# A paged-attention pipeline in which the turning of queries and keys moves from TensorE to VectorE, and projection and output products are dealt out anew over the units of a round

## The reference, cut to what matters

```python
q = rope(rmsnorm(x @ Wq.T, q_norm_w), pos)        # 32 heads of 128
k = rope(rmsnorm(x @ Wk.T, k_norm_w), pos)        # 8 heads of 128
v = x @ Wv.T
k_all = concatenate([k_cache[block_table], k])    # 512 cached keys + 32 new ones
v_all = concatenate([v_cache[block_table], v])
probs = softmax(where(valid, q @ k_all.T * SCALE, -1e30))
y = (probs @ v_all).reshape(...) @ Wo
```

## Time and profile before

| | us |
|---|---|
| median of 3 runs (3074.37 to 3078.14) | 3076.71 |
| the profiled execution | 3076.38 |
| its span, first to last instruction | 3074.7 |

### The profile page before, as it was taken

How to read it: one execution, slowest core, us unless ns; L and a number is a source line. 1 busy time by engine, 2 the same in 40 slices (tenths; PEclk the granted TensorE clock), 3 DMA queues, 4 the chain that set the end, 5 groups by cost and what they waited for, 6 DMA issues and landing times. The chain is left out here.

```text
span 3074.7 us, 54713 instructions
## 1 busy us (share of the span) xinstructions
PE 2931.6 (95%) x14616; PEld 1941.9 (63%) x14624; DVE 1527.6 (50%) x4189; ACT 1241.4 (40%) x2633; POOL 1459.5 (47%) x1262
## 2 busy tenths in 40 slices
PE   5889999999999999999999999999999998799997
PEld 3566666666666666666666666666666665455554
DVE  4544444444444444444444444444444444577675
ACT  2444444444444444444444444444444442122222
POOL 4555555555555555555555555555555551000000
PEclk9999999999999999999999999999999999899998
DMA  8544444444444444645444444444444444321110
GB/s 304 182 118 122 121 122 121 122 121 121 121 121 121 121 121 121 203 121 166 131 121 121 121 121 121 119 121 119 121 119 120 121 119 149 98 46 53 41 43 14
DMA packets 433387, 369.66 MB, mean 120 GB/s; under 512 B 90598, under 2 KB 371178, under 8 KB 432186
## 3 DMA queue, kind: packets, MB, share of 16 engines
q1 hardware_dynamic: 377834, 187.06, 21.5%
q0 software_dynamic: 48320, 165.48, 16.9%
q10 hardware_dynamic: 7056, 14.53, 1.3%
HBM read 335.66 MB, written 22.81 MB: 117 GB/s over the span
## 5 line engine op out<-in xcount | busy, mean ns | idle before, releaser
L558 DVE CUSTOM_DVE_ANT_0 ps_s<-ps_s,mask 128x544 f32<-128x544 f32 x512 | 374.9, 732 | 931.6 <-PE ps_s L388 919.3
L463 ACT ACTIVATE ps_s<-ps_s,nmax 128x544 f32<-128x544 f32 x512 | 352.3, 688 | 870.6 <-DVE nmax L558 868.4
L288 POOL DMA_INDIRECT v_sb<-in_v_rows_w,v_row x504 | 488.3, 969 | 449.6 <-PE ps_oT L416 240.5
L347 PE MATMUL ps_t<-wqkv,xT 128*128 128x512 f32 x1488 | 700.5, 593 | 0.0
L411 PEld LDWEIGHTS ps_oT<-pT,v_sb 128*128 128x128 f32 x4096 | 528.7, 192 | 192.6 <-issue 174.9
L411 PE MATMUL ps_oT<-pT,v_sb 128*128 128x128 f32 x4096 | 544.7, 276 | 12.9 <-DMA v_sb<-in_v_rows_w,v_row 12.8
L371 PE MATMUL ps_t<-wo,oT 128*128 128x512 f32 x1024 | 521.9, 594 | 1.5 <-ACT oT L477 1.2
L387 PE MATMUL ps_s<-k_sb,qT 128*128 128x416 f32 x1024 | 447.3, 519 | 19.1 <-issue 12.4
L569 DVE TENSOR_SCALAR p_sb<-ps_s,rinv 128x512 f32<-128x512 f32 x512 | 384.5, 751 | 26.9 <-DVE rinv L566 0.3
L396 PEld LDWEIGHTS ps_pT<-ident_sb,p_sb 128*128 128x128 f32 x2048 | 251.8, 141 | 187.5 <-issue 184.1
L347 PEld LDWEIGHTS ps_t<-wqkv,xT 128*128 128x128 f32 x1488 | 254.4, 191 | 178.0 <-issue 178.0
(11 more groups left out here) (224 smaller groups left out, 3305.5 us busy)
## 6 DMA issues: line engine op xcount, KB each, us to landing
k_sb<-in_kT SPq DMA_DIRECT2D x2048, 64.0 KB
v_sb<-in_v_rows_w,v_row POOLq DMA_INDIRECT x512
wo<-in_wo_w POOLq DMA_DIRECT2D x2, 4096.0 KB, 14.5
v_new<-v_raw SPq DMA_DIRECT2D x512, 16.0 KB, 1.8
y_scratch<-y_sb SPq DMA_DIRECT2D x32, 256.0 KB, 2.3
xT<-x1T_scratch POOLq DMA_DIRECT2D x31, 256.0 KB, 4.9
wqkv<-in_wqkv_w ACTq DMA_DIRECT2D x6, 1024.0 KB, 12.2
wqkv<-in_wqkv_w POOLq DMA_DIRECT2D x6, 1024.0 KB, 12.8
```

What stands on the lines that cost most here:

```text
L288: e.indirect_dma_start(out=v_sb[:, b % 2, c, :], out_offset=None, in_=A["v_rows_w"], in_offset=bass.IndirectOffsetOnAxis(ap=v_row[:, b, c: ...
L347: m = e.matmul(ps_t[bank_of(t)][:, :], xT[:, k, :], wqkv[:, k, 512 * t:512 * t + 512], start=k == 0, stop=k == KC - 1)
L463: e.activation(scores(u), scores(u), ACT.Exp, bias=nmax[:, u % 2:u % 2 + 1], scale=-1.0, accum_out=rsum[:, u % 2:u % 2 + 1]).then_inc(expe ...
L558: e.tensor_tensor_reduce(out=scores(u), in0=scores(u), in1=mask[:, b % 2, :], scale=-SCALE, scalar=3e38, op0=ALU.add, op1=ALU.min, accum_o ...
```

## The change

- **Projection** is dealt out product by product: 24 products over units 0 to 6, as 4, 3, 4, 3, 4, 3, 3 (`PROJECT_TO`), again some before and some behind `turn_p`. `DONE_AT` says in which unit each tile ends; ACT's `raw_copy` and DVE's `sums` follow one unit later.
- **Output products** stand two a unit in units 7 to 13 and one in 14 and 15. In the last round they stand two a unit in units 2 to 9.
- **Turning** leaves PE and ACT: `turn_q`, `copy_q` and the tiles `qT` and `kT_new` go. DVE turns instead: for each of the 4 sequences 4 instructions, each of which takes 32 rows and 32 columns of all 20 heads (32 x 640 elements) from `rot` to `qkT`. They stand in units 11 to 15 (two, two, one, two, one) and, of the next round, in units 0 to 2 (three, three, two), some before `norm` and some behind it.
- **`rotate`**: part 0's scale, power and product are now done tile by tile, 4 heads each, as each tile is summed. The order on POOL is otherwise as before.
- **`embed`**: the block ahead of it goes, its two loads come behind the first loads of x on SP. The projection's weights are issued by SP, one tile in each of the groups 0 to 5, in place of all six by ACT. DVE dequantises ahead of the first `spread`.
- **`tail`**: the last round's output products are made in `tail`, 11 ahead of the first transposes and 5 behind them, from `o_last`, which lies in the weights' region. The loads at its head go to POOL and split into those at once and those after the products; two of the seven instructions of `split_low_rank` go, since a mask and an identity in `B2g` let the product make the whole sum.
- The second half's projection weights count on one semaphore, so tile 0 of round 16 waits for all six.

The diff, cut to its core:

```diff
-STEPS, STEPS1 = 15, 6
+STEPS, STEPS1, RSTEPS = 17, 8, 8
+TURNS = D // S
+def blocks_turned(r, b):
+    return NQT + TURNS * GB * (r - 1) + TURNS * (b + 1)
...
-        self.qT = sb("qT", [P, 2, HKH, GB, REP, S], F32)
-        self.kT_new = sb("kT_new", [P, HKH, P], F32)
+        self.qkT = sb("qkT", [P, GB, HT, S], F32)
... rotate
-    e.wait_ge(W.summed, NQT * r + tiles)
-    e.tensor_scalar(ss[:, h0:h1], ss[:, h0:h1], 1.0 / D, EPS, ALU.mult, ALU.add).then_inc(rstd_step, 1)
-    e.tensor_tensor(rstd[:, h0:h1], ss[:, h0:h1], mhalf[:, h0:h1], ALU.pow).then_inc(rstd_step, 1)
-    e.tensor_tensor(raw[:, h0:h1, :], raw[:, h0:h1, :], rstd[:, h0:h1].unsqueeze(2).broadcast_to([P, n, D]), ALU.mult).then_inc(rope_step, 1)
+    for t0, t1 in ((0, 1), (1, 2), (2, 3)) if i == 0 else ((3, NQT),):
+        a, b = 4 * t0, 4 * t1
+        e.wait_ge(W.summed, NQT * r + t1)
+        e.tensor_scalar(ss[:, a:b], ss[:, a:b], 1.0 / D, EPS, ALU.mult, ALU.add).then_inc(rstd_step, 1)
+        e.tensor_tensor(rstd[:, a:b], ss[:, a:b], mhalf[:, a:b], ALU.pow).then_inc(rstd_step, 1)
+        e.tensor_tensor(raw[:, a:b, :], raw[:, a:b, :], rstd[:, a:b].unsqueeze(2).broadcast_to([P, b - a, D]), ALU.mult).then_inc(rope_step, 1)
... tables
-    TURN_AT = {8: 0, 9: 1, 10: 2, 11: 3, 12: 4}
-    OUT_AT = {6: (0, 2), 7: (2, 4), 8: (4, 5), 9: (5, 7), 10: (7, 8), 11: (8, 10), 12: (10, 11), 13: (11, 13), 14: (13, 14), 15: (14, 16)}
+    TURN_AT = {11: (1, 1), 12: (1, 1), 13: (1, 0), 14: (1, 1), 15: (1, 0), 0: (1, 2), 1: (1, 2), 2: (1, 1)}
+    TURN_NEXT = sum(sum(TURN_AT[u]) for u in range(11, 16))
+    PROJECT_TO = (0, 4, 7, 11, 14, 18, 21, 24)
+    DONE_AT = {u: t for t in range(NT) for u in range(7) if PROJECT_TO[u] < KC * t + KC <= PROJECT_TO[u + 1]}
+    OUT_AT = {u: (2 * u - 14, min(2 * u - 12, HQH)) for u in range(7, 14)}
+    OUT_AT.update({14: (14, 15), 15: (15, 16)})
+    LAST_OUT_AT = {u: (2 * u - 4, 2 * u - 2) for u in range(2, 2 + HQH // 2)}
... PE
+            def parts(r, n0, n1):
+                for t in range(NT):
+                    k0, k1 = max(n0 - KC * t, 0), min(n1 - KC * t, KC)
+                    if k0 < k1:
+                        project(r, t, k0, k1)
...
-                    if u < NT and not last(r):
-                        project(r + 1, u, 0, 2)
+                    if u < len(PROJECT_TO) - 1 and not last(r):
+                        half = PROJECT_TO[u] + 2
+                        parts(r + 1, PROJECT_TO[u], half)
...
-                    if u in TURN_AT and not last(r):
-                        turn_q(r + 1, TURN_AT[u])
...
-                    if u < NT and not last(r):
-                        project(r + 1, u, 2, KC)
+                    if u < len(PROJECT_TO) - 1 and not last(r):
+                        parts(r + 1, half, PROJECT_TO[u + 1])
...
-            out_product(ROUNDS - 1, 1, 0, HQH)
... ACT
-                    if 1 <= u <= NT and not last(r):
-                        raw_copy(r + 1, u - 1)
+                    if u - 1 in DONE_AT and not last(r):
+                        raw_copy(r + 1, DONE_AT[u - 1])
... DVE
+            def turn(r, m):
+                b, j = divmod(m, TURNS)
+                rows, at = slice(S * b, S * b + S), slice(S * j, S * j + S)
+                if m == 0:
+                    e.wait_ge(rope_step, STEPS * (r + 1))
+                if j == 0:
+                    e.wait_ge(scored, UNITS * (r - 1) + HKH * (b + 1))
+                    e.wait_ge(placed, GB * (r - 1) + b + 1)
+                e.transpose(qkT[at, b, :, :], rot[rows, :, at]).then_inc(q_turned, 1)
...
                         mask_scores(*ahead(r, u, 2))
-                    if 1 <= u <= NQT and not last(r):
-                        sums(r + 1, u - 1)
+                    if DONE_AT.get(u - 1, NQT) < NQT and not last(r):
+                        sums(r + 1, DONE_AT[u - 1])
                     if ahead(r, u, 1) is not None and ahead(r, u, 1)[1] % HKH == HKH - 1:
                         copy_pT(*ahead(r, u, 1))
+                    turns(r, u, 0)
                     if ahead(r, u, 2) is not None:
                         norm(*ahead(r, u, 2))
+                    turns(r, u, 1)
... tail, PE
+            out_product(0, 11)
             e.wait_ge(dma_beside, 16 * len(BESIDE))
-            e.wait_ge(padded, 1)
+            e.wait_ge(padded, 3)
             for p in both:
                 turn_a(0, p)
+            out_product(11, HQH)
... tail, split_low_rank
-                step(e.tensor_copy(td[p][own, :], bank[p][2][own, 0:P]))
-                step(e.tensor_tensor(td[p][own, :], td[p][own, :], bank[p][2][own, P:2 * P], ALU.add))
-                step(e.tensor_copy(ts[p][own, :], td[p][own, :]))
-                step(e.scalar_tensor_tensor(td[p][own, :], ts[p][own, :], part(0), td[p][own, :], ALU.mult, ALU.add))
+                t = bank[p][2][own, P:2 * P]
+                step(e.tensor_copy(ts[p][own, :], t))
+                step(e.scalar_tensor_tensor(td[p][own, :], ts[p][own, :], part(0), t, ALU.mult, ALU.add))
```

More of the change, by code:

```diff
@@ L108, in rotate @@
         if not (isinstance(r, int) and r == 0):
-            e.wait_ge(W.q_turned, NQT * r)
+            e.wait_ge(W.q_turned, blocks_turned(r - 1, GB - 1) if not (isinstance(r, int) and r == 1) else NQT)
     for a, m, t in ROPE_PARTS[i]:
@@ L517, in body @@
                         copy_pT(*ahead(r, u, 1))
-                    if u in TURN_AT and not last(r):
-                        copy_q(r + 1, TURN_AT[u], 1 - i)
             exp(0, 0)
@@ L584, in table, with turns @@
                 make_tables(e, W, csn[:, 0, :], csn[:, 1, :])
+            def turn(r, m):
[7 more added lines that the diff above has]
+                e.transpose(qkT[at, b, :, :], rot[rows, :, at]).then_inc(q_turned, 1)
+            def turns(r, u, part):
+                if u not in TURN_AT or first(r) and u < 11 or last(r) and u >= 11:
+                    return
+                units = range(11, u) if u >= 11 else range(u)
+                m = (0 if u >= 11 else TURN_NEXT) + sum(sum(TURN_AT[v]) for v in units) + part * TURN_AT[u][0]
+                for n in range(m, m + TURN_AT[u][part]):
+                    turn(r + 1 if u >= 11 else r, n)
             def body(r):
@@ L1130, in tail @@
     setup, passed, padded = sem("c_setup"), sem("c_passed"), sem("c_padded")
-    REST = 16 * (len(loads) - 1)
+    AFTER_OUT = [n for n in loads if n in after]
+    AT_ONCE = [n for n in loads if n not in after and n != "idx2"]
+    dma_after, o_done, o_copied = sem("c_dma_after"), sem("c_o_done"), sem("c_o_copied")
     chain, dma_low = sem("c_chain"), sem("c_dma_low")
@@ L1172, in _ @@
                 load(0, p)
-                e.sem_inc(stored[p], 16)
-            for n in loads:
-                if n != "idx2":
-                    e.dma_start(w[n] if n in after else w[n][:], A["c_" + n]).then_inc(dma_w, 16)
+            e.sem_inc(stored[0], 16)
+            e.wait_ge(o_copied, 1)
+            e.dma_start(y_d[ROUNDS - 1, :, :], outb[1][:, :]).then_inc(stored[1], 16)
             def store(k, p):
@@ L1208, in _, with out_product @@
                 e.wait_ge(stored[p], 16 * (I_STEPS + 1))
+        @block.gpsimd
+        def _(e):
+            for p in both:
+                e.dma_start(A2g[p][:, :, TR0:P], A["c_w2f"][:, :, P + TR0:FOLDED]).then_inc(dma_low, 16)
+            for n in AT_ONCE:
+                e.dma_start(w[n][:], A["c_" + n]).then_inc(dma_w, 16)
+            e.wait_ge(o_done, 1)
+            for n in AFTER_OUT:
+                e.dma_start(w[n], A["c_" + n]).then_inc(dma_after, 16)
         @block.tensor
         def _(e):
+            def out_product(h0, h1):
+                for h in range(h0, h1):
+                    m = e.matmul(bank[1][3][:, :], o_last[:, h, :], wo[:, h, :], start=h == 0, stop=h == HQH - 1)
+                if h1 == HQH:
+                    m.then_inc(o_done, 1)
             def turn4(k, p, src, ready, done, id_=ident, to=None):
@@ L1436, in _ @@
             e.wait_ge(padded, 1)
-            HEAD, CH = 30, 54
+            for p in both:
+                e.tensor_copy(B2g[p][TR0:P, P + TR0:FOLDED], ident[TR0:P, TR0:P]).then_inc(padded, 1)
+            HEAD, CH = 26, 50
             done = [0]
```

157 lines of the change are left out of this document (72 added, 85 removed).

## The result

| | before | changed |
|---|---|---|
| median, us | 3075.54 (4 runs, 3072.82 to 3078.14) | 3109.98 (4 runs, 3103.18 to 3120.96) |
| ratio | 1 | 1.0115 (95% interval 1.0084 to 1.0147) |
| span of the profiled execution | 3074.7 | 3110.3 |

The change makes the kernel 1.15% slower, 34 us. The forecast was 3091.

A forecast was written before the change was run, and what follows sets the result against it. PE, 95% busy, was taken to bound the kernel, with the values' gathers just in time. The sum: 3076.4 + 51 + 5 + 4 + 1 - 25 - 10 - 11 = 3091 us, range 3054 to 3148.

The forecast's parts named there:

- Turning on PE, -2.2 a round: Five `turn_q` of 0.44 leave PE in each round, saving 2.2 us one to one.
- DVE's turns, 0.9 each and covered: Units 11 to 15: eight DVE turns make 15.9 us of DVE work, hidden beside PE's 19.7.
- The wait for `rope_step`: DVE's wait in unit 11: about even, a few tenths covered by DVE's 3.8 us to spare.
- The upper bound: Rival: a DVE turn costs 1.9, units 11 to 15 overrun, +36 us in all, so 3127; chance 0.10.
- Unit 3, +0.9: PE's product 12 waits for DVE's sum of tile 1: 0.83 a round, about +0.9 with the semaphore.
- Unit 12, +3.0: PE's `weigh` waits 3.2 for values gathered later since tile 2 ends later; 0.2 was there, so +3.0 a round.
- near 95: Sign in the profile: `weigh` in unit 12 waits for `v_sb` some 30 times, near 95 us in all.
- The ends: Outside the rounds: -25 behind the last round, -10 in `split_low_rank`, -11 in `embed`.
- the sum of a round: Ordinary round: -2.2 + 0.9 + 3.0 = +1.7 us, in 30 rounds +51.
- a rival: PE's clock falls after each unit 12 wait: 1.8 a round, +53 in all, so 3144; chance 0.15.
- the likeliest case: Whole kernel: 3091 us, own range 3074 to 3108, chance 0.48.
- Round 16, +1: Tile 0's wait for all six weight tiles is mostly given back by an existing 3.24 wait: +1 (0 to +4).

The follow-up runs named there:

- first experiment: Against the changed kernel, projection dealt out as 4 products a unit in units 0 to 5 again: 2943.58 us, ratio 0.9558 to the kernel before.
- second experiment: Against the changed kernel, projection bounds moved so tile 1 ends in unit 1 and tile 2 still in unit 3: 3085.05 us.
- third experiment: Against the changed kernel, fourth sequence's gathers issued ahead of part 1 of the rotation, DVE's turns begun in unit 12 instead of 11: 3094.73 us.

## Why the prediction was right, and where its sum was off

The direction, the mechanism and the place were right: the queries' and keys' turning gives 2.2 a round, and two waits take it back. By its steps:

- **Turning on PE, -2.2 a round:** right, 2.18 by the run that put 20 transposes back. The rule of the Trainium skill that the prediction named (page "VectorE: DVE Perf Modes", section "Rules for kernel authors"), that a 128x128 turning belongs on TensorE where PSUM will do, doesn't hold here: TensorE is the bound, and VectorE's 16 turns cost nothing where they stand. The same run gives the change's worth of the turning, 91 us with the stops.
- **DVE's turns, 0.9 each and covered:** right, 0.836, and PE full for a whole round with them (first experiment). The wait for `rope_step` didn't show either. The upper bound was wrong: at twice the price it isn't units 11 to 15 alone that are too long, and it costs 7.6 a round, not 1.2 (the run with doubled turns; it has no wait for values to hide in).
- **Unit 3, +0.9:** right, 0.83 in each of 31 rounds. The second experiment, without it, is 25 us faster, though other terms moved there too.
- **Unit 12, +3.0:** right in its chain, and a little high. The marks on POOL lie about 0.2 us or less from the forecast; PE waited 2.8 a round, and the list has 84.7 us (87.0 with the last round) where "near 95" was said. The prediction took two long waits off the old ones, 4.1 and 3.24; they are one, at 1290.56, listed for PEld and for PE, which changes its count by 0.1. Waits for K pages hardly showed (2.5 us, twice); the third experiment has them just behind.
- **The ends:** embed -9.3 for -11, the tail's whole -40.2 for -35. PE's waits for the split fell from 10.3 us (11 times) to 0.3 (once), and the experiment that made the chain seven long again confirms them. In `embed` PE's wait behind the weight tiles fell from 7.1 to 2.9 and its first wait, for `bd`, from 19.0 to 16.6; no run separates the two. The stretch between the last `weigh` and the first step's transposes fell from 56 to 31 us, PE now being busy for 27.45 of it against 29.23 of 56.
- **What failed: the sum of a round,** +1.7. Measured in the 29 ordinary rounds between the marks (without the one that brings new weights, 82.56 and 86.79): (78.1 - 4.2) / 29 = +2.55. Two terms weren't in it. The clock behind the waits cost 0.9 a round (25 us in 29). It had been priced rightly as a rival (1.8 a time, for mostly 1.7) and left out of the likeliest case, as if it had to fall always or never. On the other side, the stops of PE's loop went, which the prediction hadn't seen although the kernel before has them (ten of 0.9 to 1.5 us): its rounds average 77.4, 0.15 of this being its waits for values, while the undisturbed one is 76.6. The sum with both, -2.2 + 0.8 + 2.6 + 0.9 - 0.6 = +1.5, still falls short of 2.55 by 1.0. Of it 0.2 is PE's new `issue` gaps (7.1 us), 0.2 the waits for `k_sb` and `p_sb`, 0.3 that the first products behind each wait take 0.1 to 0.2 longer at full clock too, and 0.1 that some products near unit 8 take 0.3 longer in many rounds. About 0.2 a round stays open, and these shares are read from rows, not separated by a run.
- **Round 16, +1:** right. It came to +4.2 in all, 1.7 more than an ordinary round. PE now waits 5.7 for the six weight tiles, 41 us behind the mark; the old wait of 3.24 for values stood 44 behind it and is gone, so it was given back.

With the projection in fours, the same turning and ends are 4.4% faster than the kernel before. All of the loss hangs on the bounds of the projection's parts, which are worth 166 us. The forecast was 19 us low: 26 by the rounds, of which the tail gave 5 back. That the loop's stops went, 0.6 a round or some 18 us, was unforeseen and hid half of the miss: that part of its closeness is luck.

## What to carry to other kernels

Work that is moved to even out an engine's units moves the end of each of its pieces too: follow the last piece to the slowest chain that starts from it, here 32 us of instructions and a gather on another engine, before looking at the units. A wait on the bounding engine is to be priced twice, by its length and by the clock behind it; the second isn't "each time or never", since here slow products followed nearly none, some or all of the waits of one kind, by their length. And shortening such a chain by moving a transfer isn't the same as shortening it, since the transfer may meet another one.

## What the runs showed of the hardware

- **PE's clock and a wait:** behind waits for values under 2.3 us products were slow once in 66 times, behind those of 3.5 and over each time (29), and between them 36 of 58 times, mostly at 1.7 us each. With DVE doubled, waits of 1.9 to 2.0 for DVE were followed by slow products 22 of 29 times, so the length of the one wait doesn't decide alone.
- **Fetching a loop:** PE's loops of two rounds stopped 0.9 to 2.3 us at each new pass, with 137 or 138 instruction packets, and with 40 fewer PE turnings in a pass not at all, with 46. With 20 fewer it stopped in one of two loops, with 92. The profile puts the stop down to `issue` or to an instruction of DVE that had long been done. That the packets are the cause is argued from their number, not shown.
- **DVE's turning** of 32 x 640 f32 took 827 to 842 ns, hardly more than a pass over 512 columns on 128 partitions, 0.75.
